# Seven fp32 projections of a fused transformer kernel as three fp32r products of high and low parts

## The reference

```python
x = x + xattn(layernorm(x), ctx)         # q = xn@Wq; softmax(q k^T/8) v; @Wo + bo
xn = layernorm(layernorm(x)) * g + b
w = sigmoid(xn @ Wx @ Ww + bw); k = xn @ Wk; v = xn @ Wv; r = sigmoid(xn @ Wr)
state = (1 - w) * state + k v^T;  out = r . state       # scan over 32 tokens
x = x + out @ Wo2
x = x + gelu(layernorm(x) @ U1 @ V1 + b1) @ U2 @ V2 + b2
```

## Time and profile before

| what | value |
|---|---|
| median of 3 runs | 1066.17 us |
| the profiled execution | 1066.57 us |
| its span | 1064.8 us |
| mean granted TensorE clock | 0.995 |
| PE busy | 1032.9 us, 97% of the span |
| weight loads busy | 813.2 us, 76% |
| ACT busy | 588.1 us, 55% |
| DVE busy | 447.5 us, 42% |
| POOL busy | 206.8 us, 19% |

### The profile page before, as it was taken

How to read it: one execution, slowest core, us unless ns; L and a number is a source line. 1 busy time by engine, 2 the same in 40 slices (tenths; PEclk the granted TensorE clock), 3 DMA queues, 4 the chain that set the end, 5 groups by cost and what they waited for, 6 DMA issues and landing times.

```text
span 1064.8 us, 20023 instructions
## 1 busy us (share of the span) xinstructions
PE 1032.9 (97%) x7742; PEld 813.2 (76%) x7742; DVE 447.5 (42%) x1065; ACT 588.1 (55%) x1402; POOL 206.8 (19%) x356
## 2 busy tenths in 40 slices
PE   4899999999999999999999999999999999999997
PEld 2577878787887877788777878777787787877775
DVE  3233544362453526245352633535254353426142
ACT  2354547466473745647375574746557474664531
POOL 0010303022030302204031130303113031211230
PEclk9999999999999999999999999999999999999999
DMA  8232222112222222222212222221222222122000
GB/s 280 73 109 80 82 62 82 60 57 82 81 82 72 65 70 64 74 91 70 83 54 79 65 74 90 65 90 50 70 77 75 81 64 73 49 76 81 2 11 20
DMA packets 57996, 78.94 MB, mean 74 GB/s; under 512 B 10288, under 2 KB 39856, under 8 KB 57904
## 3 DMA queue, kind: packets, MB, share of 16 engines
q1 hardware_dynamic: 54304, 72.71, 22.3%
q10 hardware_dynamic: 3600, 4.96, 1.3%
HBM read 73.18 MB, written 4.46 MB: 73 GB/s over the span
## 4 chain that ended last, share of the span: by engine, by line
PE 89%; issue 3%; DVE 2%; ACT 2%; POOL 2%; ACTq 1%; SPq 1%; DMA 0%; POOLq 0%; DVEq 0%
PE scores L353 10%; PE scores L356 7%; PE gb L451 7%; PE acc L382 7%; PE acc L378 6%; PE gb L415 6%; PE gb L439 5%; PE gb L328 5%; PE ptp L365 5%; PE gb L339 5%; PE gb L471 5%; PE acc L383 5%; PE gb L519 3%; PE gb L509 2%; PE gb L458 2%
## 5 line engine op out<-in xcount | busy, mean ns | idle before, releaser
L714 DVE TENSOR_REDUCE nmax<-scores 128x2 f32<-128x514 f32 x128 | 88.7, 693 | 335.9 <-PE scores L356 335.1
L582 ACT ACTIVATE probs<-scores,nmax 128x257 f32<-128x257 f32 x256 | 119.8, 474 | 178.1 <-DVE nmax L714 177.9
L860 POOL TENSOR_TENSOR ptm<-probs,head 128x32 f32<-128x32 f32 x128 | 32.3, 252 | 616.4 <-DVE probs L721 616.4
L353 PE MATMUL scores<-raw_t,qk 128*128 128x257 f32 x512 | 133.0, 383 | 1.5 <-ACT qk L614 1.2
L353 PEld LDWEIGHTS scores<-raw_t,qk 128*128 128x128 f32 x512 | 87.6, 191 | 9.0 <-issue 1.6
L721 DVE TENSOR_TENSOR probs<-probs,rinv 128x514 f32<-128x514 f32 x128 | 88.9, 695 | 4.4
L356 PE MATMUL scores<-raw_t,qk 64*128 64x257 f32 x512 | 90.7, 431 | 0.0
L382 PE MATMUL acc<-pt,raw_n 128*128 128x256 f32 x256 | 90.0, 433 | 0.0
L378 PE MATMUL acc<-pt,raw_n 128*64 128x128 f32 x1024 | 83.5, 284 | 0.8 <-ACT pt L587 0.8
L378 PEld LDWEIGHTS acc<-pt,raw_n 128*64 128x64 f32 x1024 | 56.0, 137 | 36.4 <-issue 32.6
L365 PE MATMUL ptp<-ident,probs 128*128 128x128 f32 x512 | 77.7, 274 | 6.0 <-DVE probs L721 5.9
(11 more groups left out here) (110 smaller groups left out, 1942.0 us busy)
## 6 DMA issues: line engine op xcount, KB each, us to landing
raw_t<-in_ctx_t SPq DMA_DIRECT2D x128, 258.0 KB, 2.8
raw_n<-in_ctx_n SPq DMA_DIRECT2D x128, 192.0 KB, 2.4
xin<-in_x SPq DMA_DIRECT2D x16, 256.0 KB, 2.8
xb<-in_x SPq DMA_DIRECT2D x16, 256.0 KB, 2.7
vsp<-tail_values SPq DMA_DIRECT2D x256, 2.0 KB
out<-ob SPq DMA_DIRECT2D x16, 256.0 KB, 2.2
wq<-in_wq ACTq DMA_DIRECT2D x1, 512.0 KB, 4.4
wk<-in_wk SPq DMA_DIRECT2D x1, 512.0 KB, 5.4
```

Of the source, the lines that this page charges most:

```text
L353: mm(scores[:, r, 0:L], w[:, 0, b, r * P:(r + 1) * P], x[:, 0, 0:L], start=True, stop=False)
L582: go(probs[n % 2][:, r, 0:L], scores[:, r, 0:L], ACT.Exp, bias=nmax[:, r:r + 1], accum_out=rsum[:, r:r + 1]).then_inc(s["exp_ready"], 1)
L714: v_.tensor_reduce(nmax[:], scores[:, :, 0:L], AX.X, ALU.max, negate=True)\
```

## The change

Each of the matmuls of q, z, k, r, v, Y1 and Y2 is written out as three matmuls in the type float32r: high part by high part, low by high, and high by low. The order on PE of all else stays. The new helper `terms` issues them (L324 of the changed kernel).

For the data operand ACT writes the high part where it wrote the evacuated tile before (a copy into a float32r tile), and DVE writes the low part, tile minus high part, in a new step that waits for ACT. XT2 keeps its float32 copy in SBUF (`xt2`), from which a further ACT copy makes the high part and a DVE subtraction the low part. A bank is now released by DVE's subtraction for XT, WV0, WV1, O2 and WZ. The weights come from DRAM into `qk[1]` and are split once by DVE: `wq` ahead of the loop, the others after slots (0, 0), (0, 1) and (0, 2); the clearing of `vsp`, `s2`, `su`, `inv`, `khat` moves from ahead of the loop to slot (-1, 3). ACT waits for all weights at slot (0, 3).

```diff
+            def terms(out_, factors):
+                products = [(w, x) for (w_h, w_l), (x_h, x_l) in factors
+                            for w, x in ((w_h, x_h), (w_l, x_h), (w_h, x_l))]
+                for k, (w, x) in enumerate(products):
+                    last = mm(out_, w, x, start=k == 0, stop=k == len(products) - 1)
+                return last
...
                 if name == "z":
-                    drained("XT2", g)
+                    pe.wait_ge(s["xt2_l_ready"], g + 1)
...
                 for o in range(2):
-                    for c in range(2):
-                        last = mm(out_[:, o], w[:, c, o * P:(o + 1) * P], xt2[:, c], start=c == 0, stop=c == 1)
+                    o_ = slice(o * P, (o + 1) * P)
+                    last = terms(out_[:, o], [((w_h[:, c, o_], w_l[:, c, o_]), (xt2_h[:, c], xt2_l[:, c]))
+                                              for c in range(2)])
...
                     if n == "XT":
-                        drain(n, g, go(xt1[:], t[:], ACT.Copy))
+                        go(xt1_h[:], t[:], ACT.Copy).then_inc(s["xt1_h_ready"], 1)
                     elif n == "XT2":
...
                         drain(n, g, last)
+                        bank, k = BANK["XT2", g]
+                        act.wait_ge(bank_drained[bank], k)
+                        go(xt2_h[:], xt2[:], ACT.Copy).then_inc(s["xt2_h_ready"], 1)
...
                     elif n == "O2":
-                        drain(n, g, go(o2[:], t[:], ACT.Copy))
+                        go(o2_h[:], t[:], ACT.Copy).then_inc(s["o2_h_ready"], 1)
...
+                elif n == "XT":
+                    t = wait_tile(n, g)
+                    dve.wait_ge(s["xt1_h_ready"], g + 1)
+                    drain(n, g, v_.tensor_tensor(xt1_l[:], t[:], xt1_h[:].bitcast(F32), ALU.subtract))
+                elif n == "XT2":
+                    dve.wait_ge(s["xt2_h_ready"], g + 1)
+                    v_.tensor_tensor(xt2_l[:], xt2[:], xt2_h[:].bitcast(F32), ALU.subtract)\
+                        .then_inc(s["xt2_l_ready"], 1)
...
-            GAPS = [[["psp-1"], [], ["S2-2", "S3-2"]],
-                    [[], [], ["Y3-3", "Y1-1"]],
-                    [["xn1-1"], [], []],
-                    [["Y2-2"], ["xn2-2"], []],
+            GAPS = [[["psp-1"], [], ["S2-2", "S3-2", "WV0-1", "WV1-1"]],
+                    [[], [], ["O2-2", "Y3-3", "Y1-1"]],
+                    [["XT+1", "xn1-1"], [], []],
+                    [["Y2-2"], ["XT2-1", "xn2-2"], []],
...
+            def split(raw, hi, lo, then=None):
+                link(v_.tensor_copy(hi, raw))
+                last = v_.tensor_tensor(lo, raw, hi.bitcast(F32), ALU.subtract)
...
+            dve.wait_ge(wq_in, 16)
+            split(wq_raw, wq_h[:].rearrange(whole), wq_l[:].rearrange(whole), s["wq_ready"])
...
+                    if (i, b) == (FIRST, 3):
+                        constants()
+                    if (i, b) == (0, 0):
+                        dve.wait_ge(wb_in, W_B)
+                        split(w2_raw[:, 0:1024], *(x[:, 0:1024] for x in w2_parts))
+                    if (i, b) == (0, 1):
+                        split(wo_raw, wo_h[:].rearrange(whole), wo_l[:].rearrange(whole))
+                    if (i, b) == (0, 2):
+                        split(w2_raw[:, 1024:1536], *(x[:, 1024:1536] for x in w2_parts))
+                        split(wo2_raw, wo2_h[:].rearrange(whole), wo2_l[:].rearrange(whole), s["weights_ready"])
```

More of the change, by code:

```diff
@@ L7 @@
 F32 = mybir.dt.float32
+F32R = mybir.dt.float32r
 U8 = mybir.dt.uint8
@@ L181, in build @@
         s2 = sb("s2", [P, 8, P])
-        o2 = sb("o2", [P, 2, T])
+        o2_h, o2_l = (sb(n, [P, 2, T], F32R) for n in ("o2_h", "o2_l"))
         xn2, xt3 = sb("xn2", [P, 2, D]), sb("xt3", [P, 2, T])
@@ L325, in q @@
                 if g == 0 and p == 0:
-                    pe.wait_ge(wq_in, 16)
-                for c in range(2):
-                    last = mm(out_[:, 0], wq[:, c, p * P:(p + 1) * P], xt1[:, c], start=c == 0, stop=c == 1)
+                    pe.wait_ge(s["wq_ready"], 1)
+                p_ = slice(p * P, (p + 1) * P)
+                last = terms(out_[:, 0], [((wq_h[:, c, p_], wq_l[:, c, p_]), (xt1_h[:, c], xt1_l[:, c]))
+                                          for c in range(2)])
                 done(f"q{p}", g, last)
@@ L435, in y1 @@
                 drained("WV1", g)
+                if g == 0:
+                    pe.wait_ge(s["weights_ready"], 1)
                 for t in range(2):
                     t_ = slice(t * P, (t + 1) * P)
-                    for p in range(4):
-                        last = mm(out_[:, t], o_[:, p, t_], wo[:, p], start=p == 0, stop=p == 3)
+                    last = terms(out_[:, t], [((o_h[:, p, t_], o_l[:, p, t_]), (wo_h[:, p], wo_l[:, p]))
+                                              for p in range(4)])
                 done("Y1", g, last)
             def project(name, g):
-                w = {"z": wz, "k": w2[:, 0], "r": w2[:, 2]}[name]
+                w_h, w_l = {"z": (wz_h, wz_l), "k": (w2_h[:, 0], w2_l[:, 0]), "r": (w2_h[:, 2], w2_l[:, 2])}[name]
                 out_ = tile(name, g)
                 if name == "z":
-                    drained("XT2", g)
+                    pe.wait_ge(s["xt2_l_ready"], g + 1)
                     if g == 0:
@@ L456, in v @@
                 for t in range(2):
-                    for c in range(2):
-                        last = mm(out_[:, t], xt2[:, c, t * P:(t + 1) * P], w2[:, 1, c], start=c == 0, stop=c == 1)
+                    t_ = slice(t * P, (t + 1) * P)
+                    last = terms(out_[:, t], [((xt2_h[:, c, t_], xt2_l[:, c, t_]), (w2_h[:, 1, c], w2_l[:, 1, c]))
+                                              for c in range(2)])
                 done("v", g, last)
@@ L492, in y2 @@
                 for t in range(2):
-                    for c in range(2):
-                        last = mm(out_[:, t], o2[:, c, t * P:(t + 1) * P], wo2[:, c], start=c == 0, stop=c == 1)
+                    t_ = slice(t * P, (t + 1) * P)
+                    last = terms(out_[:, t], [((o2_h[:, c, t_], o2_l[:, c, t_]), (wo2_h[:, c], wo2_l[:, c]))
+                                              for c in range(2)])
                 done("Y2", g, last)
@@ L544, in stay_busy @@
                 for k in range(count):
-                    mm(scores[:, 0, 0:256], ident[:], wq[:, 0, 0:256], start=True, stop=True)
+                    mm(scores[:, 0, 0:256], ident[:], v1[:, 0:256], start=True, stop=True)
             pe.wait_ge(id_in, 16)
@@ L659, in _ @@
                         act.wait_ge(s["small_ready"], 1)
+                    if i == 0 and b == 3:
+                        act.wait_ge(s["weights_ready"], 1)
                     if 0 <= n < B:
```

78 lines of the change are left out of this document (52 added, 26 removed).

## The result

The changed kernel takes 1033.2 us (median of 4 runs, 1030.28 to 1036.50) against 1066.23 in the same comparison: ratio 0.9686, interval 0.9665 to 0.9708. A second comparison with more runs gives 1028.73 (1028.18 to 1033.67, 5 runs) against 1066.91, ratio 0.9655, 0.9630 to 0.9681. Forecast were 1021 us and a range of 1006 to 1050: the sign, the mechanism and the range hold, the median lies 8 to 12 us above the forecast. The second comparison was expected at 1030 to 1037 us and came out lower, with three of its five executions at a mean granted clock of 0.998. Executions with the same mean clock differ less: at 0.998 the kernel before takes 1063.16 to 1063.80 us in that comparison and the changed one 1028.18 to 1028.73, some 35 us apart.

A forecast was written before the change was run, and what follows sets the result against it. PE's own work was taken as the bound: 58.8 us gained there, less 7.4 for waits in slots 4 to 6, 4.0 not gained, 0.2 at the start and 2.2 at the end, gave 1021 us, range 1006 to 1050.

The forecast's parts named there:

- What bounds the kernel: In the full groups only PE's own work sets the pace: busy 864.93 of 865 us from 85 to 950 us.
- The pace of float32r: In the seven projections each float32r instruction takes 110 ns, so PE gains 58.8 us.
- above 120 ns: Sign on the chain in L324: a pace above this per instruction would show the forecast wrong.
- a case of 120 ns: Slow edge of the likeliest case for the new PE matmuls: 17 us less gained, 1037 us.
- The first rival: On PE, float32r moves a column in two clocks like fp32, 216 ns an instruction: 1193 us; chance 0.10.
- the fourth: On PE, float32r is assembled as full float32, 432 ns for each of 1728: 1564 us; chance 0.01.
- the second: On PE, the weight load no longer hides, 130 ns an instruction: 1050 us; chance 0.08.
- Slots 4 to 6: PE waits for `probs` before the next transposes, giving back 0.57 us a group, 7.4 us in 13 groups.
- Slots 1 to 3: The added high and low parts on ACT and DVE fit into existing room and cost nothing.
- Start and end: First slots +0.2 us; last group +2.2 us, from the new handovers before z (+1.4) and Y2 (+0.8).
- The sum: Whole kernel: -58.8 + 7.4 + 4.0 + 0.2 + 2.2 = -45.0 us, giving 1021 us.

The follow-up runs named there:

- e_hh_fp32: The changed kernel with each product one fp32 matmul of the high parts, low parts still made and waited for: 1067.86 us against 1066.76, ratio 1.0011.

## Why the prediction was right, and where it was off

**What bounds the kernel.** Right: after the change PE is busy for 833.30 of 835 us, and a period follows PE's work.

**The pace of float32r.** The term that was mis-sized. I took 110 ns, from four clocks a column shared among four partial products plus the 2 to 3 ns of fp32. The column rate is right: from 256 to 512 columns float32r goes from 119.7 to 227.5 ns, 107.8 for 256 columns. The constant is not: it is 13 ns and belongs to the type. In the kernel 118 ns make a gain of 248.8 - 1728 x 0.118 = 44.9 us in place of 58.8, so 13.9 less. PE's busy time in the execution with the clock at 0.998 is 988.2 us, 44.7 below; that the two agree so well is in part chance, since the execution of before had 0.995. The forecast named "above 120 ns" as what would prove it wrong and a case of 120 ns as the edge of its own range; at 118 the edge was nearly reached. The first rival (216 ns) and the fourth are out, and the second (130 ns) is met by two fifths. Its reason, a load that no longer hides, is not borne out: with 512 columns the constant is the same, and with 32-column weights too. The second half of that reason, a fixed handover between load and matmul, is not excluded. A floor shows only below some 230 columns, an estimate from (111 - 13.5) x 2.4 = 234; that this floor is the weight load was not tested.

**Slots 4 to 6.** The mechanism is right, link by link. PE's work shrank by 36 x 0.078 = 2.81 us in a group and the period by 2.52, so 0.29 are given back, not 0.57. The prediction's own working gives this with the pace as measured: k, q3, r and v save (4 + 2 + 4 + 4) x 0.078 = 1.09 us and not 1.43, PE reaches the transposes at 560.46 - 1.09 = 559.37 and waits until 559.60, 0.23 us. So this error followed from the first. The timeline of PE after the change has the wait at this place:

```profile
543.11 0.28 PE L324 MATMUL gb<-w_l,xt_h 128*128 128x256 f32 x1
543.47 0.66 PE L381 MATMUL ptp<-ident,probs 128*128 128x128 f32 x4
```

The first is v's last matmul; a next one would have begun 0.12 us later, at 543.23, and the transposes begin at 543.47, so they are 0.24 us late. Over 13 groups the 0.29 us are 3.7 in place of 7.4. The other 0.05 us of a group are within the rounding of the 118 ns.

**Slots 1 to 3.** Right; e_hh_fp32 has the period unchanged with every handover in place, and in the changed kernel the waits listed for PE between 85 and 920 us are for `probs` alone. In the timeline of DVE the low parts of the two WV tiles stand in idle time, and the next `nmax` waits for PE alone:

```profile
559.93 1.29 DVE L790 TENSOR_TENSOR o_l<-gb,o_h 128x512 fp32r<-128x512 f32 x2 [4.23 <-ACT o_h L641]
563.13 0.69 DVE L740 TENSOR_REDUCE nmax<-scores 128x2 f32<-128x514 f32 x1 [1.91 <-PE scores L372]
```

The rows that were added on DVE sum to 62 us (64 forecast); its busy time rises by 56, since neighbours overlap by some 0.1 us. ACT has 10.1 us of new rows as forecast and, for the same reason, only 6.5 more of busy time.

**Start and end.** The handovers cost what was said: in the last group z begins 1.52 us after XT2's evacuation and 0.14 before, +1.4 as forecast, by these two links of the chain:

```profile
991.41 0.64 ACT xt_h L631
992.07 0.70 DVE xt_l L783
```

What the prediction did not have is the clock at both ends. In the profiled execution of after 1.2 GHz reaches over some 10 us at the start and again over the heaviest tile of the last group; before, the window from 30 to 36 us and one from 998 to 1008 had some of it too (0.87, 0.56 and 0.83). The changed kernel loses the clock more often: four of its nine executions had a mean of 0.988 to 0.993, while the 42 executions of the kernel before whose clock is on record beside the experiments had 0.994 to 0.998. Less work on PE is not needed for it: e_hh_fp32, with the work of before and the new handovers, fell to 0.992 in two of ten, and in its profiled execution, after 0.50 from 998 to 1008 us, the tile of 48 matmuls takes 5.55 us. So the new handovers can come with it; what share PE's shorter work has was not tested.

**The sum.** With the two sizes set right it is -45.0 + 13.9 - 3.7 = -34.8 us. The medians have -33.0 and -38.2, the profiled executions -30.1 (clock 0.988) and -38.4 (0.998), the last three of these four against a clock of 0.995 before; at the same mean clock of 0.998 it is about -35. The twelve full periods, which no clock disturbs, have -30.3 us. PE's saving alone, 12 x 2.81 = 33.7, leaves 3.4 of it given back, which is 0.29 in each. So the pace of float32r, net of the smaller wait, makes 10 of the us that the forecast missed, which would be 1031 us; the medians lie 2 us above and 3 below that, on the two sides that their mean clocks have (0.992 to 0.993 and 0.998).

## What to carry to other kernels

A price that the trace cannot show is best split into a slope and a constant, and each bounded by itself: here the slope came out of the trace within 1%, and the constant, taken over from another type, cost a quarter of the distance to the break-even (8 of 34 ns). When one engine is relieved in small steps, ask at which step the next engine's chain ties with it; a chain that suddenly changes engine while the first one stays 99.8% busy marks the tie, not a loss. And before mixing types to save a few ns per matmul, count the changes of type.

## What the runs showed of the hardware

- float32r with 128 x 128 weights: columns / 2.4 GHz + 12 to 14 ns for 256 to 512 columns, 111 ns flat for 128 and 192; bf16: + 2.5 to 3 ns (109.7 at 256, 215.9 at 512); fp32: two instructions of 215.8 ns for 256 columns, 218.9 with other weights.
- A change between float32r and bf16 and back costs 15 to 16 ns; between float32r and fp32 none was seen (551 ns for 119 + 432).
- float32r with 64 rows in place of 128 takes 126 ns, 6 more than with 128.
- bf16 data read with a 4-byte step: 113.4 ns in place of 109.1; weights so read: 109.1.
- DVE casts 1024 columns of float32 to float32r in SBUF in 0.69 us, below the 0.9 to 1.4 that I allowed, and subtracts 1024 columns in 1.22.
